# Depthwise and output products in halves of the rows inside a window-attention loop, and the next image's statistics in the projection stage

## The reference, cut to what matters

```python
x = x + L0(_gn(x), W_qkv, b_qkv, lepe_w, lepe_b, W_o, b_o)   # _gn: GroupNorm, 32 groups of 4 channels
# L0: 7 x 7 windows of 8 x 8 pixels, 8 heads of 16 channels
proj = xw @ W_qkv + b_qkv
q, kv = proj[..., :128], proj[..., 128:]
lepe = conv3x3_depthwise(v_img, lepe_w) + lepe_b             # on the whole image of v
logit = einsum('npc,nqc->npq', mean(q) * SCALE, mean(k))     # window means
r_idx = top_k(logit, 4)                                      # 4 windows of keys for each window
attn = softmax(q_h * SCALE @ k_sel.T)                        # 64 queries x 256 keys a head
o = attn @ v_sel
out = (o + lepe) @ W_o + b_o
```

## Time and profile before

| what | value |
|---|---|
| median of 3 runs | 3900.28 us (3899.26 to 3907.92) |
| the profiled execution | 3898.74 us, span 3897.0 us |
| busy in the span | PE 90%, DVE 64%, ACT 56%, POOL 47% |
| mean granted TensorE clock | 0.969 of full |
| first turn of the attention loop, first and last image | 69.31 us, 1526.02 us |

### The profile page before, as it was taken

How to read it: one execution, slowest core, us unless ns; L and a number is a source line. 1 busy time by engine, 2 the same in 40 slices (tenths; PEclk the granted TensorE clock), 3 DMA queues, 4 the chain that set the end, 5 groups by cost and what they waited for, 6 DMA issues and landing times. The chain is left out here.

```text
span 3897.0 us, 106851 instructions
## 1 busy us (share of the span) xinstructions
PE 3509.7 (90%) x30516; PEld 2922.8 (75%) x30516; DVE 2500.8 (64%) x6153; ACT 2177.0 (56%) x5985; POOL 1837.3 (47%) x2998
## 2 busy tenths in 40 slices
PE   6989898888889898969999999999999968779998
PEld 3555555555555555559999999999999967779888
DVE  4868687777868686853333333333333389989998
ACT  4878787887878787844443333333333334345554
POOL 2747374655647474720003333333334457756665
PEclk9999999999999999989999999999999979989999
DMA  6232222223131323211110000000012100000000
GB/s 214 63 96 71 88 78 90 76 63 97 53 111 51 110 56 103 64 65 48 48 49 0 0 0 0 0 0 0 0 33 64 43 10 1 1 19 28 34 34 34
DMA packets 202728, 194.25 MB, mean 50 GB/s; under 512 B 35728, under 2 KB 190992, under 8 KB 199312
## 3 DMA queue, kind: packets, MB, share of 16 engines
q1 hardware_dynamic: 171024, 177.08, 14.6%
q10 hardware_dynamic: 31360, 12.87, 1.2%
HBM read 123.24 MB, written 66.58 MB: 49 GB/s over the span
## 5 line engine op out<-in xcount | busy, mean ns | idle before, releaser
L196 PE MATMUL bank<-h,w_hh 128*128 128x128 f32 x8032 | 933.8, 275 | 0.0
L196 PEld LDWEIGHTS bank<-h,w_hh 128*128 128x128 f32 x8032 | 917.1, 192 | 0.0
L1567 ACT ACTIVATE Pr<-bank,nmx 128x256 f32<-128x256 f32 x1568 | 721.0, 472 | 191.5 <-DVE nmx L1666 187.9
L241 ACT ACTIVATE h<-bank,bg 128x128 f32<-128x128 f32 x1008 | 370.0, 367 | 818.7 <-PE bank L196 818.6
L1504 POOL TENSOR_TENSOR Pr<-Pr,rden 128x512 f32<-128x512 f32 (+1 forms) x784 | 660.5, 853 | 182.6 <-DVE rden L1726 135.8
L1666 DVE TENSOR_REDUCE nmx<-bank 128x1 f32<-128x256 f32 x1568 | 553.8, 414 | 96.5 <-PE bank L1829 92.5
L1494 POOL COPY kg<-kT 128x64 f32 x1568 | 303.1, 237 | 535.0 <-DMA row<-ix 299.6
L287 DVE SCALAR_TENSOR_TENSOR inp<-bank,b_in,tz 128x256 f32<-128x256 f32 x196 | 85.8, 479 | 697.5 <-ACT tz L224 697.5
L260 POOL CAST h_hi<-h 128x512 fp32r<-128x512 f32 x196 | 119.7, 611 | 685.6 <-ACT h L241 685.6
L1829 PE MATMUL bank<-kg,qT 32*128 32x256 f32 x3136 | 410.3, 440 | 31.1 <-POOL kg L1494 22.3
L1576 ACT ACTIVATE PT<-bank 128x512 f32<-128x512 f32 x784 | 428.1, 609 | 15.9 <-PE bank L1842 15.7
(11 more groups left out here) (253 smaller groups left out, 6600.1 us busy)
## 6 DMA issues: line engine op xcount, KB each, us to landing
v_rows<-v_padded SPq DMA_DIRECT2D x168, 232.0 KB, 3.3
vg<-v_windows SPq DMA_DIRECT2D x1176, 32.0 KB, 2.1
first_gates<-gate_sums SPq DMA_DIRECT2D x28, 512.0 KB, 2.6
gate_sums<-first_gates SPq DMA_DIRECT2D x28, 512.0 KB, 3.6
v_padded<-vpad SPq DMA_DIRECT2D x56, 232.0 KB, 2.3
X<-in_x SPq DMA_DIRECT2D x8, 1568.0 KB, 15.1
vg<-v_windows ACTq DMA_DIRECT2D x392, 32.0 KB, 2.2
x_backup<-X SPq DMA_DIRECT2D x8, 1568.0 KB, 6.0
```

The costliest lines, as they stand in the source:

```text
L196: ins = pe.matmul(bank[m][:, tt * COLS:(tt + 1) * COLS], w_hh[:, k, m * 128:(m + 1) * 128], prev[:, k, :], start=False, stop=(k == NH - 1) ...
L241: act.activation(h[:, 2 * q + tt, m, :], bank[m][:, tt * COLS:(tt + 1) * COLS], ACT.Tanh, bias=bg[:, 0, m:m + 1]).then_inc(s_h, 1)
L1567: act.activation(Pr[:, par, j, :], bank[j][:, 0:KEYS], ACT.Exp, bias=nmx[:, par, j:j + 1], accum_out=den[:, par, j:j + 1])\
```

## The change

Depthwise units and output products are cut in two halves of four rows (224 columns). A table `FILL_AT` places them: output halves at w = 7(b+1)+2 and +3, depthwise halves at w = 7(b-2)+4, 5, 6, 7, 7, 8 (block 2: 5, 6, 6, 7, 7, 8), so most windows have one and every seventh has two. The next image's seven bn_stats move to the qkv stage, one behind each block's v; their aggregation to w = 6. The mean's matmul moves from w = 33 to 39 and DVE's steps on it to 40; the variance's matmul stays at 40 and DVE's step goes to 41. The second image gets a load semaphore of its own. The waits on bank 7 stay what they were, at the new places.

```diff
-            OUT_LAG, ADD_LAG = 3, 4
-            STATS_AT = {13: 0, 15: 1, 20: 2, 22: 3, 27: 4, 29: 5, 30: 6}
-            MEAN_AT, VAR_AT = 33, 40
-
-            LEPE_AT = {NWIN * (b - 2) + 6 + dx: (b, dx) for b in range(2, NBLK) for dx in range(3)}
+            ADD_LAG = 4
+            MEAN_AT, VAR_AT = 39, 40
+
+            HALF = BLK // 2
+            FILL_AT = {w: [] for w in range(P2)}
+            for b in range(NBLK - 1):
+                for h in range(2):
+                    FILL_AT[NWIN * (b + 1) + 2 + h].append(("out", b, 0, h))
+            for b in range(2, NBLK):
+                for i, w in enumerate((4, 5, 6, 7, 7, 8) if b > 2 else (5, 6, 6, 7, 7, 8)):
+                    FILL_AT[NWIN * (b - 2) + w].append(("lepe", b, i // 2, i % 2))
...
+                            if more:
+                                if b == 0:
+                                    dve.wait_ge(s_ldx[1], 16)
+                                input_stats(dve, following(n), b)
...
-                            if more and w in STATS_AT:
-                                if w == min(STATS_AT):
-                                    dve.wait_ge(s_ldx[1], 16 * (B - 1))
-                                input_stats(dve, following(n), STATS_AT[w])
-                            if more and w == max(STATS_AT) + 1:
+                            if more and w == NWIN - 1:
+                                dve.wait_ge(s_ldx[2], 16 * (B - 2))
                                 input_aggregate(dve, following(n))
-                            if more and w == MEAN_AT:
+                            if more and w == MEAN_AT + 1:
                                 input_mean(dve, following(n))
-                            if more and w == VAR_AT:
+                            if more and w == VAR_AT + 1:
                                 input_var(dve, following(n))
...
-                        def out(b):
-                            pe.wait_ge(s_o, n * P2 + (b + 1) * NWIN + 1)
-                            if b + 2 < NBLK:
-                                pe.wait_ge(s_le, n * NBLK + b + 3)
-                            else:
-                                pe.wait_ge(s_ev, n * NBLK + b + 1)
-                            pe.matmul(bank[7][:, 0:BLK], w_o[:], by_row(oT[:, b % 2, :]), start=True, stop=True)\
-                                .then_inc(s_out, 1)
+                        def out(b, h):
+                            if h == 0:
+                                pe.wait_ge(s_o, n * P2 + (b + 1) * NWIN + 1)
+                                if b + 2 < NBLK:
+                                    pe.wait_ge(s_le, n * NBLK + b + 3)
+                                else:
+                                    pe.wait_ge(s_ev, n * NBLK + b + 1)
+                            ins = pe.matmul(bank[7][:, h * HALF:(h + 1) * HALF], w_o[:],
+                                            by_row(oT[:, b % 2, :])[:, h * ROWS // 2:(h + 1) * ROWS // 2],
+                                            start=(h == 0), stop=(h == 1))
+                            if h:
+                                ins.then_inc(s_out, 1)
...
+                            for what, b, dx, h in FILL_AT[w]:
+                                if what == "out":
+                                    if more and b == NBLK - 2 and h == 0:
+                                        pe.wait_ge(s_id, following(n) * IN_DVE + 4)
+                                    out(b, h)
+                                else:
+                                    if dx == 0 and h == 0:
+                                        if b == 2:
+                                            pe.wait_ge(s_le, n * NBLK + 2)
+                                        else:
+                                            pe.wait_ge(s_ev, n * NBLK + b - 1)
+                                    lepe(b, dx, h, bank[7])
```

More of the change, by code:

```diff
@@ L1230, in program @@
             sb, _, sem = mk(c0)
-            s_ldx = [sem("first_image_loaded"), sem("images_loaded")]
+            s_ldx = [sem("first_image_loaded"), sem("second_image_loaded"), sem("images_loaded")]
             s_ib, s_ia = sem("input_block_stats"), sem("input_aggregated")
@@ L1384, in _ @@
                     for n in range(1, B):
-                        sp.dma_start(X[:, n * HW:(n + 1) * HW], x_in[n]).then_inc(s_ldx[1], 16)
+                        sp.dma_start(X[:, n * HW:(n + 1) * HW], x_in[n]).then_inc(s_ldx[min(n, 2)], 16)
                     sp.wait_ge(s_padz, BORDERS)
@@ L1792, in image, with lepe @@
                         pe.wait_ge(s_v, n * NBLK + NBLK)
-                        def lepe(b, dx, to):
-                            if dx == 0:
+                        def lepe(b, dx, h, to):
+                            if dx == 0 and h == 0:
                                 loads = 4 - b % 2
@@ L1799, in lepe @@
                             for i in range(STRIPS):
-                                ins = pe.matmul(to[STRIP * i:STRIP * i + STRIP, 0:BLK], w_tap[:, dx * STRIPS + i, :],
-                                                vrow[:, b % 2, i, :, dx:dx + W], start=(dx == 0), stop=(dx == 2))
-                            if dx == 2:
-                                ins.then_inc(s_lp, 1)
-                        def out(b):
-                            pe.wait_ge(s_o, n * P2 + (b + 1) * NWIN + 1)
-                            if b + 2 < NBLK:
-                                pe.wait_ge(s_le, n * NBLK + b + 3)
-                            else:
-                                pe.wait_ge(s_ev, n * NBLK + b + 1)
-                            pe.matmul(bank[7][:, 0:BLK], w_o[:], by_row(oT[:, b % 2, :]), start=True, stop=True)\
-                                .then_inc(s_out, 1)
@@ L1814, in image @@
-                        for dx in range(3):
-                            lepe(0, dx, bank[7])
+                                ins = pe.matmul(to[STRIP * i:STRIP * i + STRIP, h * HALF:(h + 1) * HALF],
+                                                w_tap[:, dx * STRIPS + i, :],
+                                                vrow[:, b % 2, i, h * ROWS // 2:(h + 1) * ROWS // 2, dx:dx + W],
+                                                start=(dx == 0 and h == 0), stop=(dx == 2 and h == 1))
+                            if dx == 2 and h == 1:
+                                ins.then_inc(s_lp, 1)
@@ L1816, in image @@
+                        for i in range(6):
+                            lepe(0, i // 2, i % 2, bank[7])
                         pe.wait_ge(s_k, n * NBLK + NBLK)
@@ L1818, in image @@
                         pe.matmul(bank[1][0:P2, 0:P2], qs[:], ks[:], start=True, stop=True).then_inc(s_lg, 1)
-                        for dx in range(3):
-                            lepe(1, dx, bank[6])
+                        for i in range(6):
+                            lepe(1, i // 2, i % 2, bank[6])
                         pe.wait_ge(s_tk, n * 3 + 2)
@@ L1864, in fill @@
                         def fill(w):
[L1866 to L1872, removed]
-                                    pe.wait_ge(s_ev, n * NBLK + b - 1)
-                                lepe(b, dx, bank[7])
-                            b, lag = divmod(w - NWIN, NWIN)
-                            if b >= 0 and lag == OUT_LAG:
-                                out(b)
+                            for what, b, dx, h in FILL_AT[w]:
[4 more added lines that the diff above has]
+                                else:
+                                    if dx == 0 and h == 0:
+                                        if b == 2:
[3 more added lines that the diff above has]
+                                    lepe(b, dx, h, bank[7])
                             if more and w in (MEAN_AT, VAR_AT):
-                                pe.wait_ge(s_ev, n * NBLK + b + 2)
+                                pe.wait_ge(s_ev, n * NBLK + (w - NWIN) // NWIN + 2)
                                 if w == MEAN_AT:
@@ L1892, in image @@
                         attend(P2 - 1, 0, (P2 - 1) % 3, (P2 - 1) // 3)
-                        out(NBLK - 1)
+                        out(NBLK - 1, 0)
+                        out(NBLK - 1, 1)
                     with pe.Fori(0, B - 1) as n:
```

2 lines of the change are left out of this document (1 added, 1 removed).

## The result

The changed kernel takes 3953.77 us (median of 4 runs, 3952.32 to 3958.54), the kernel before on the same chip 3900.13: ratio 1.0135, interval 1.0118 to 1.0153. It is slower by 53.6 us; 3939 was forecast, and 3953.8 lies inside the range of 3914 to 3962. The profiled execution, the slowest of the four, has a span of 3956.8 us. Of the experiments' executions one, of the kernel without the normalisation's waits, took 4125.73 us at a granted clock of 0.831; it is left out, and the time given for that kernel is the median of its other three.

A forecast was written before the change was run, and what follows sets the result against it. No engine share names the bound; PE's fills and DVE's extras alternate lap by lap. Per image 5.5 - 0.4 - 0.5 + 0.3 + 0.1 = +5.0, 35 for seven, +4 for the last: +39 on 3900.3, 3939 us, range 3914 to 3962.

The forecast's parts named there:

- The rules: Attention loop, second image: lap timings read from trace rows, such as DVE's max-to-max lap of at least 2.96 us.
- The copy's wake-up: Output half waiting for DVE's lepe copy: 0.06 us to wake, then 0.48 to the scores.
- e(w) = m(w) + 0.46: Every loop window w: ACT's first exp starts 0.46 us after the first of DVE's four maxes.
- Rival 3: PE's clock falls to half in the waits: 4049 us, or some 10 if once per image; chance 0.06.
- signs of being wrong: In the loop: no PE idle at the named waits, laps under 3.5, or a granted clock under 1.00.
- Rival 2: Waits come, but ACT and DVE running ahead in later windows take half of each back: 3903 us; chance 0.08.
- The 0.50 for one half: Depthwise half alone, from its start to the next scores: 0.50 us, against 0.88 for a whole unit.
- The 0.3 per image for the six halves ahead of the logits: Six depthwise halves ahead of the logits: 6 x 0.45 against 2.4, +0.3 us per image.
- rival 4: Statistics not hidden in the qkv stretch: at most +4.3 us per image on top, 3969 us; chance 0.03.
- Rival 1: Waits find inputs ready and smoothing wins: some 3.6 us less per image, 3870 us; chance 0.06.
- m(16) of 22.75: Middle stretch without waits: window 16's max comes 22.75 us after window 9's, 0.7 below before.
- 5.5 - 0.4 - 0.5 + 0.1: Per image: +5.5 windows 9 to 44, -0.4 windows 5 to 9, -0.5 windows 44 to 48, +0.1 last output product.

## Why the prediction was right and wrong

**Direction and mechanism.** Eleven waits of PE for DVE on bank 7 and on the normalisation, in the windows named, with the releasers named; taking them away, alone and together, takes the loss away. That step is shown.

**The laps of a middle block**, forecast and measured in the second image:

| from max to max | 9 to 10 | 10 to 11 | 11 to 12 | 12 to 13 | 13 to 14 | 14 to 15 | 15 to 16 | sum |
|---|---|---|---|---|---|---|---|---|
| forecast | 4.12 | 2.96 | 4.31 | 3.17 | 3.09 | 3.83 | 2.96 | 24.44 |
| measured | 4.27 | 3.04 | 4.25 | 3.18 | 3.11 | 3.75 | 2.97 | 24.57 |

The rules held to 0.15 each. The copy's wake-up was mis-sized: 0.15 from the end of the copy to the output half, not 0.06 (which no row had shown), and 0.54 from that half to the scores, not 0.48; the lap behind a wait is 3.04, not 2.96. The add's was over-sized, 0.13 for 0.20. Four stretches are 98.2 against 97.8 forecast. PE's idle time was forecast at about 1.2 and 1.3 and measured at 0.7 to 1.0 and 0.6 to 0.9: the attend group, 0.09 ahead of the max in the earlier trace rows, starts 0.34 behind it here, and PE is done later. The laps hold all the same, since they hang on the end of DVE's step and not on when PE is free.

**Windows 37 to 44** are where the forecast fell short most: 25.25 to 25.73 measured, 25.44 in the mean of seven images, 24.5 forecast, 22.7 before. The waits came out as said: windows 39 and 40 took 4.03 and 4.42 against 4.0 and 4.45, and the copy's lap of window 37 has its 0.14 of late wake-up again. The failed step is what "the same rules" make of the windows behind: e(w) = m(w) + 0.46 doesn't hold in window 43. ACT there, changed kernel (the max was at 435.43):

```profile
434.68 1.08 ACT L1582 ACTIVATE PT<-bank 128x512 f32<-128x512 f32 x2
435.25 0.49 ACTq L1375 DMA_DIRECT2D vg<-v_windows  x1
436.34 0.47 ACT L1573 ACTIVATE Pr<-bank,nmx 128x256 f32<-128x256 f32 x1 [0.58 <-DVE nmx L1676]
```

The exp comes 0.91 behind, in this window of each of the seven images (0.91 to 1.03), and just so in the kernel before, where the forecast's own trace could have shown it (0.94 in the second image, 416.71 to 417.65). The next lap is 3.43 where 2.96 was taken. I had read the rule in windows 8 and 9 and used it for 35 windows more.

The trace also has what holds the exp. ACT's program is a loop of six windows a pass, `act.Fori(0, (P2 - 1) // 6)`, so a new pass begins in windows 7, 13, 19, 25, 31, 37 and 43, and its register and branch instructions stand ahead of the first exp (source view, 290 to 440 us; durations in ns, then the first and last start):

```profile
L1606 ACTq COMPARE_BRANCH  x7: 53/53/53, 308.1 to 435.8; - x7
```

From the first of them to the exp 0.56 us pass. In the six earlier windows they begin 0.3 to 1.0 ahead of the max and are over in time (exp 0.45 or 0.46 behind the max). In window 43 they begin 0.35 behind it, at 435.78, and the exp starts at 436.34. In the kernel before they begin 0.38 behind the max there, and 0.02 behind it in window 13, whose exp comes 0.57 late. Why ACT itself is late in window 43 was not followed further. That lap is some 0.5 of the 0.94 by which windows 37 to 44 fell short; the rest is the clock's fall in the first two images, the laps behind a wait and the late wake-up.

**Rival 3**, the clock, came in its mild form and in less of it: two falls in seven images, 0.4 each, where 10 us per run was its price; behind the ten other waits of an image the clock stayed at 1.00. A granted clock under 1.00 in the loop stood among the signs of being wrong; it was seen, though the laps say that the rest of the mechanism held. How near the rival was is seen in the three kernels that keep the normalisation's waits and have fewer others: the fall came there in 20 of 21 images. The rule of the Trainium skill cited there (TensorE: Matmul & The Clock Gate, A second HAM failure mode) would have the clock swing between its rates in such a loop. This trace agrees behind the longest wait, in two images, and not behind the waits of 0.55 to 0.95, which are the frequent ones.

**Rival 2** had ACT and DVE take half of each wait back. They don't: the lap behind the copy's wait is 3.04, and taking the waits out gave back all that they had cost.

**What the halves give** came out as forecast in windows 5 to 9 (13.39, 0.36 less) and in 44 to 48 (0.3 to 0.4 less against 0.5). The 0.50 for one half was 0.52. The 0.3 per image for the six halves ahead of the logits was nothing: in the second image they take 2.41 to the logits and three whole units took 2.39. The rule cited for the halves (the Trainium skill, TensorE: Matmul & The Clock Gate, Back-to-back issue gap) would, by the estimate made from it, have one half cost 0.44; the row has 0.52, so the term from the rows was the nearer one.

**The statistics** cost nothing that the times show, as said, and rival 4 falls with it. Rival 1 would have had the matmuls find their inputs ready; PE waited eleven times. Its other half was tried: with all waits gone the smoothing should have been worth 3.6 us per image by that rival's working, and the loops give 1.0 to 1.4, the time 0.5. Its m(16) of 22.75 was called 0.7 below before; it measured 22.94, and before it was 23.28, so a stretch gives 0.34.

**The sum.** Loops: forecast 5.5 - 0.4 - 0.5 + 0.1 = 4.7 per image and 4 for the last, 37 in all; measured 48.3. The missing 11 are windows 37 to 44 (0.94 x 7 = 6.6 us) and the four stretches (0.4 x 7 = 2.9), and small differences for the rest. That 53.6 still falls in the range is in part luck: its bounds were worked out from the size of a half, the wake-up and the rivals, and none of them covers window 43. Outside the loops 2 were forecast. The profiled execution shows 4.5 at the start, 4.1 in the gaps, 2.9 in the later layers, but the kernels that share its code there have starts of 69.4 to 72.3, and the medians differ by 53.6, not 59.8. In its start PE waited longer for the v images, and what came behind ran at half clock:

```profile
59.90 3.34 PE L1807 MATMUL bank<-v_rows,w_tap 96*32 96x224 f32 x48 [2.78 <-ACT vst L1544]
63.17 0.40 PE L1831 MATMUL bank<-ks,qs 128*49 128x49 f32 x2
63.51 4.71 PE L1807 MATMUL bank<-v_rows,w_tap 96*32 96x224 f32 x48
```

Before, the idle time was 1.89, and both runs took 2.46. That is a piece of this execution and not of the change as far as the other kernels show. Why the rest of the program, whose code is the same, took 2217.3 here and 2219.3 in one experiment against 2214.4 to 2216.5 elsewhere stays open.

## What to carry to other kernels

Where one PSUM bank is handed from engine to engine inside a software pipeline, the product that takes it over belongs one lap behind the step that frees it: half a unit moved one window early, into the lap of that step, cost 0.5 to 0.7 us each time here, though the half itself cost 0.5 and PE had the room. Smoothing the work of an engine that is 90% busy gains only in laps that this engine bounds; look for them lap by lap before cutting anything. And price a wait by the lap that it makes, not by its idle time: taking one away made the next one longer.

## What the hardware showed that was not expected

- Four kernels have the two waits of the normalisation, 0.6 to 1.2 us and then, where the clock is up, 1.5 to 1.6 us with PE busy 0.44 of 2 us in the changed kernel. In 22 of their 28 images with these waits the granted clock fell to 0.50 near them, in the changed kernel in only 2 of 7; in the eight executions without them it did so in none of 56. What decides between a fall and none in the changed kernel stays open.
- ACT's loop of six windows a pass puts 0.56 us ahead of the first exp of each pass. That is hidden in six passes of an image and shows in the seventh, window 43: its first exp comes 0.91 to 1.03 us behind the first max in the first seven images of the changed kernel, 0.94 or 0.95 in the kernel before, 0.45 in most other windows.
- From the end of DVE's copy to the matmul that waits for it 0.15 us pass, where 0.06 was taken, and from the end of its add 0.13.
- Cutting each group of 448 columns in two adjacent ones of 224 is free: eight loops of 1280.2 in sum against 1279.5 and 1280.0.
- Two executions of the kernel before have loops within 0.5 us of each other in 1280, while the stages with transfers between them differ by 3.6 in 334. The two of the version without waits differ by 2.9 in their loops, with the granted clock at the loop's start. Both are read window by window from the trace, far more sharply than from the time.
